# The first stage of a fused attention and feed-forward kernel, in 256-token chunks

## What is computed

```python
xn = layernorm(x)
q_c  = rms_norm(xn @ wq_down.T, q_norm_w)       # 1536 wide
kv_c = rms_norm(xn @ wkv_down.T, kv_norm_w)     # 512 wide
k_rope = rope(xn @ wk_rope.T)                   # 64 wide
q, k, v = up-projections of q_c and kv_c, 16 heads
s = softmax(causal(q k^T * scale)) v @ wo.T
g = silu(down(silu(gate(xn) * gate_s) * (up(xn) * up_s)) * down_s)
out = x + s * g
```

## Time and profile before

| | us |
|---|---|
| runs shown (3) | 4663.2, 4666.9, 4667.2; median 4666.9 |
| the profiled execution | 4694.8 |
| its span, slowest core (7) | 4693.3 |
| first stage on that core | 0 to 573.4 |
| its first matmul | 94.8 |

### The profile page before, as it was taken

One profiled execution on the slowest core, in us unless ns is written; L12 is line 12 of the kernel. 1 busy time (PEld: TensorE's weight loads), 2 busy tenths in 40 slices (PEclk: granted clock), 3 DMA queues, 4 the chain that ended last, 5 costly groups with the idle time before them and its releaser, 6 DMA issues.

```text
span 4693.3 us, 57615 instructions; the slowest of 8 cores (4635.0 to 4693.3 us)
## 1 busy us (share of the span) xinstructions
PE 3775.5 (80%) x22128; PEld 1896.8 (40%) x22128; DVE 1598.3 (34%) x3298; ACT 1205.3 (26%) x1751; POOL 365.6 (8%) x455
## 2 busy tenths in 40 slices
PE   1777796766676667756775999999799999999998
PEld 0333343444344444434442444444344444444443
DVE  2444335665565556655673111110000111110100
ACT  1222104544454445545552000000000111000000
POOL 0111230000000000000000000000000100000101
PEclk9887798998898888988998999999899999999999
DMA  8555246787878787788777344445655443434564
GB/s 180 137 139 139 61 110 104 116 116 115 101 121 116 116 109 119 111 106 113 121 118 180 72 78 75 78 74 176 190 189 194 84 81 72 81 72 135 175 197 157
DMA packets 778331, 566.60 MB, mean 121 GB/s; under 512 B 689232, under 2 KB 697680, under 8 KB 766928
## 3 DMA queue, kind: packets, MB, share of 16 engines
q1 hardware_dynamic: 711840, 318.04, 35.3%
q0 software_dynamic: 37424, 171.46, 20.2%
q10 hardware_dynamic: 28800, 73.41, 5.1%
HBM read 499.34 MB, written 73.40 MB: 122 GB/s over the span
## 4 chain that ended last, share of the span: by engine, by line
PE 65%; DMA 16%; DVE 12%; issue 3%; ACT 2%; another core or an unknown queue 1%; SPq 0%; POOL 0%; ACTq 0%; DVEq 0%; POOLq 0%
PE bk L1065 25%; PE bk L1085 11%; DMA pt<-pp 8%; DVE nmx L895 6%; PE bk L1104 5%; PE ps_mm L427 4%; PE ps_u L829 4%; PE ps_o L883 3%; PE ps_s L862 3%; DMA dw<-d 3%; PE ps_s L865 3%; PE ps_kv L427 2%; PE ps_u L834 2%; PE ps_r L665 2%; DMA xt<-xn 2%
## 5 line engine op out<-in xcount | busy, mean ns | idle before, releaser
L939 ACT ACTIVATE pp<-ps_s,bia,scq 128x1024 bf16<-128x1024 f32 (+3 forms) x640 | 690.1, 1078 | 861.0 <-DMA pt<-pp 345.6
L895 DVE TENSOR_REDUCE nmx<-ps_s 128x1 f32<-128x1024 f32 (+3 forms) x640 | 680.3, 1063 | 665.8 <-PE ps_s L869 436.5
L883 PE MATMUL ps_o<-vv,pt 128*128 128x129 bf16 x4352 | 370.1, 226 | 471.8 <-DMA pt<-pp 327.6
L1065 PE MATMUL bk<-xc,gw 128*128 128x512 bf16 x2816 | 643.0, 382 | 48.5 <-DMA uw<-upP 48.5
L1085 PE MATMUL bk<-dw,hdn 128*128 128x512 bf16 x2816 | 616.7, 381 | 56.1 <-DMA dw<-d 53.9
L1065 PE MATMUL bk<-xc,uw 128*128 128x512 bf16 x2816 | 636.5, 379 | 0.0
L883 PEld LDWEIGHTS ps_o<-vv,pt 128*128 128x128 bf16 x4352 | 287.0, 100 | 631.9 <-issue 607.4
L1121 DVE SCALAR_TENSOR_TENSOR hdn<-bk,us_s,sg 128x512 bf16<-128x512 f32 x176 | 132.1, 751 | 1137.7 <-PE bk L1065 1061.5
L1085 PEld LDWEIGHTS bk<-dw,hdn 128*128 128x128 bf16 x2816 | 275.8, 98 | 395.1 <-issue 69.2
L1065 PEld LDWEIGHTS bk<-xc,gw 128*128 128x128 bf16 x2816 | 276.9, 98 | 386.1 <-issue 58.2
L862 PE MATMUL ps_s<-kk,qn 128*128 128x512 bf16 (+3 forms) x1280 | 349.2, 355 | 97.0 <-ACT fac L944 86.8
(11 more groups left out here) (101 smaller groups left out, 2696.2 us busy)
## 6 DMA issues: line engine op xcount, KB each, us to landing
dw<-d SPq DMA_DIRECT2D x176, 512.0 KB, 4.6
gw<-gateP POOLq DMA_DIRECT2D x88, 512.0 KB, 5.1
uw<-upP POOLq DMA_DIRECT2D x88, 512.0 KB, 7.1
xb<-xk ACTq DMA_DIRECT2D x32, 1024.0 KB, 6.4
wo_s<-wo SPq DMA_DIRECT2D x16, 2048.0 KB, 9.6
d<-downP POOLq DMA_DIRECT2D x16, 1408.0 KB, 22.1
xo<-xk ACTq DMA_DIRECT2D x64, 256.0 KB, 4.9
out<-xo ACTq DMA_DIRECT2D x64, 256.0 KB, 6.1
```

Of the source, the lines that this page charges most:

```text
L883: mm_ = e.matmul(ps_o[n % 2][:, 0:129], pt[n % NPT][:, j * 128:(j + 1) * 128], V[:, kt, 0:129], start=(j == 0), stop=(j == 2 * nt - 1))
L895: kb.go(e, lambda: e.tensor_reduce(nmx[n % 8][:], r3(ps_s[n % 2][:], 2)[:, :, 0:w], AX.XY, ALU.max, negate=True), [("p", f"b_s_{n}")], "v")
L939: kb.go(e, lambda: e.activation(r3(pp[n % NP][:, 0:2 * w], 2), r3(ps_s[n % 2][:], 2)[:, :, 0:w], AF.Exp, bias=bia[n % 8][:], scale=scq[:, ...
L1065: mm_ = e.matmul(bk[pr * 2 + z][:], W[u_i % 2][:, dc * 128:(dc + 1) * 128], xc[hf][:, dc * 512:(dc + 1) * 512], start=(dc == 0), stop=(dc ...
```

## The change

The chunks of the first stage become 256 tokens wide, 16 in number, two tiles each. `CSEQ` starts with two kv-only chunks and then alternates, with two own chunks at the end. There are four `xt`, three `xb`. Layer norm runs three chunks ahead: six tiles stand before the first job, and chunk n carries the tiles of chunk n + 3. A query or kv job makes two groups of 128 outputs side by side in one bank, 16 matmuls of 256 columns each, so a job still has 512 columns of result; own chunks have 6 query jobs, all have 2 kv jobs and a rope job of 256 columns. The kv squares are summed by TensorE over two accumulators rather than added by POOL. The statistics are handed on from chunk to chunk, one event behind each job: a kv-only chunk carries qc and qd of the own chunk before and its own kc; its kd and ka follow the first and second job of the next chunk; an own chunk has kc after its rope job, kd after the fourth query job, ka after the fifth. `rb` is the same buffer as `dg`. SP loads x, the constants and the rotary factors, x first; a later x load stands on SP behind the transpose of the tile three before. The query weights come in six pieces, each with a semaphore of its own. Stores to DRAM are in pieces of 256 tokens, 512 bytes each. VectorE waits for the constants only where it needs them.

```diff
-    w["wqd"] = _tiles(a(inputs["L0_attn_wq_down"]).T, 128, QR)
+    w["wqd"] = _tiles(a(inputs["L0_attn_wq_down"]).T, 128, 256)
...
-            xb = [sb(f"xb{i}", [128, D], F32) for i in range(2)]
+            xb = [sb(f"xb{i}", [128, D], F32) for i in range(NX)]
             xn = [sb(f"xn{i}", [128, D], BF16) for i in range(2)]
-            xt = [sb(f"xt{i}", [128, NDC * 512], BF16) for i in range(2)]
...
-            acck = sb("acck", [128, 512], F32)
+            acck = [sb(f"acck{i}", [128, 512], F32) for i in range(2)]
             accq = sb("accq", [128, 512], F32)
-            cs = [sb(f"cs{i}", [128, 512], F32) for i in range(2)]
-            dg = sb("dg", [128, 512], F32)
-            rb = sb("rb", [128, 512], F32)
...
-            CSEQ = [0, 4, 1, 5, 2, 6, 3, 7]
+
+            CSEQ = [8, 9, 0, 10, 1, 11, 2, 12, 3, 13, 4, 14, 5, 15, 6, 7]
+            NC = len(CSEQ)
+            LNS = 2 * NC
 
             def sched():
                 ev = []
-                for t in range(4):
-                    ev += [("L1", 0, t), ("L2", 0, t)]
+                for n in range(3):
+                    for t in range(2):
+                        ev += [("L1", n, t), ("L2", n, t)]
+                late = []
                 for n, c in enumerate(CSEQ):
...
+                    jobs = ([("q", 0), ("q", 1), ("q", 2), ("kv", 0), ("kv", 1), ("kr", 0),
+                             ("q", 3), ("q", 4), ("q", 5)] if c < 8 else [("kv", 0), ("kv", 1), ("kr", 0)])
+                    todo = []
+                    if n + 3 < NC:
+                        for t in range(2):
+                            todo += [[("L1", n + 3, t)], [("L2", n + 3, t)]]
+                    stats, late = late, []
                     for j, job in enumerate(jobs):
                         ev.append(("job", n, job))
...
+                        if job == ("kr", 0):
+                            stats += [("kc", n), ("kd", n), ("ka", n)]
+                        for _ in range(2 if c >= 8 else 1):
+                            if todo:
+                                ev += todo.pop(0)
+                        if stats:
+                            ev.append(stats.pop(0))
+                    for left in todo:
+                        ev += left
+                    late = stats + ([("qc", n), ("qd", n)] if c < 8 else [])
+                return ev + late
...
                 if job[0] == "kv":
-                    return ps_kv[job[1]]
+                    return ps_kv[(n % 2) * 2 + job[1]]
...
             def a_sync(e):
+                def load(tt):
+                    row = CSEQ[tt // 2] * 256 + (tt % 2) * 128
+                    kb.inc(e.dma_start(out=xb[tt % NX][:], in_=xk_d[row:row + 128, :]), f"xb{tt % NX}", 16)
+                    kb.mark(f"a_x_{tt}", f"xb{tt % NX}")
...
+                for tt in range(NX):
+                    load(tt)
...
+                load_cs(0)
+                load_cs(1)
                 for ev_ in EV:
+                    if ev_[0] == "job" and ev_[2][0] == "kr" and 0 < ev_[1] < NC - 1:
+                        kb.wait(e, "v", f"a_kro_{ev_[1] - 1}")
+                        load_cs(ev_[1] + 1)
                     if ev_[0] != "L2":
                         continue
                     _, n, t = ev_
-                    sl = (n * 4 + t) % 2
+                    tt = n * 2 + t
                     kb.wait(e, "a", f"a_xn_{n}_{t}")
-                    kb.wait(e, "p", f"a_jobs_{n - 2}")
-                    kb.wait(e, f"xst{((n - 2) // 2) % 2}", f"a_xst_{n - 2}")
-                    xt_ = f"xt{n % 2}{t}"
+                    kb.wait(e, "p", f"a_jobs_{n - 4}")
+                    kb.wait(e, f"xst{(n // 2) % 2}", f"a_xst_{n - 4}")
+                    xt_ = f"xt{n % 4}{t}"
                     kb.inc(e.dma_start_transpose(
-                        out=r3(xt[n % 2][:], NDC)[:, :, t * 128:(t + 1) * 128],
-                        in_=xn[sl][:]), xt_, 16)
+                        out=r3(xt[n % 4][:], NDC)[:, :, t * 128:(t + 1) * 128],
+                        in_=xn[tt % 2][:]), xt_, 16)
                     kb.mark(f"a_xt_{n}_{t}", xt_)
+                    if tt + NX < LNS:
+                        load(tt + NX)
...
-                H = NDC * QR // 4
-                for z in range(4):
-                    kb.inc(e.dma_start(out=wqd[:, z * H:(z + 1) * H], in_=wqd_d[:, z * H:(z + 1) * H]),
-                           "wa1", 16)
-                kb.mark("a_wq", "wa1")
+                H = NDC * 256
+                for z in range(6):
+                    kb.inc(e.dma_start(out=wqd[:, z * H:(z + 1) * H], in_=wqd_d[z * 128:(z + 1) * 128, :]),
+                           f"wq{z}", 16)
+                    kb.mark(f"a_wq_{z}", f"wq{z}")
                 for ev_ in EV:
                     if ev_[0] == "job":
                         _, n, job = ev_
...
+                        if r == 2:
+                            for t in range(2):
+                                kb.wait(e, f"xt{n % 4}{t}", f"a_xt_{n}_{t}")
+                            c = CSEQ[n]
+                            dst = r3(xnscr[(c // 2) * 128:(c // 2 + 1) * 128, :], NDC)
+                            s_ = f"xst{(n // 2) % 2}"
+                            kb.wait(e, s_, f"a_xst_{n - 4}")
+                            kb.inc(e.dma_start(out=dst[:, :, (c % 2) * 256:(c % 2 + 1) * 256],
+                                               in_=r3(xt[n % 4][:], NDC)), s_, 16)
+                            kb.mark(f"a_xst_{n}", s_)
...
                         if job[0] == "q":
-                            kb.wait(e, "wa1", "a_wq")
+                            kb.wait(e, f"wq{job[1]}", f"a_wq_{job[1]}")
                         if job[0] == "kv":
-                            kb.wait(e, "v", f"a_ka_{n - 1}")
+                            kb.wait(e, "v", f"a_ka_{n - 2}")
...
+                        X = xt[n % 4]
+                        for z in range(1 if job[0] == "kr" else 2):
+                            for dc in range(NDC):
+                                if job[0] == "kv":
+                                    k0 = dc * KVR + (job[1] * 2 + z) * 128
+                                    wt = wkvd[:, k0:k0 + 128]
+                                elif job[0] == "kr":
+                                    wt = wkr[:, dc * 128:(dc + 1) * 128]
+                                else:
+                                    k0 = job[1] * NDC * 256 + dc * 256 + z * 128
+                                    wt = wqd[:, k0:k0 + 128]
+                                mm_ = e.matmul(bk[:, z * 256:(z + 1) * 256], wt, X[:, dc * 256:(dc + 1) * 256],
+                                               start=(dc == 0), stop=(dc == NDC - 1))
...
+                        if ev_[0] == "kc":
+                            kb.wait(e, "a", f"a_sq_{n}_kv_1")
+                            parts = [(acck[0], 0), (acck[0], 1), (acck[1], 0), (acck[1], 1)]
                         else:
-                            kb.wait(e, "a", f"a_rb_{n - 1}")
-                            kb.wait(e, "v", f"a_qu_{n - 1}")
-                        for tt in range(4):
-                            mm_ = e.matmul(ps_st[:, tt:tt + 1], acc[:, tt * 128:(tt + 1) * 128], ones[:, 0:1],
-                                           start=True, stop=True)
+                            kb.wait(e, "g", f"a_add_{n}_5")
+                            parts = [(accq, 0), (accq, 1)]
+                        for tt in range(2):
+                            for k, (acc, z) in enumerate(parts):
+                                k0 = z * 256 + tt * 128
+                                mm_ = e.matmul(ps_st[:, tt:tt + 1], acc[:, k0:k0 + 128], ones[:, 0:1],
+                                               start=(k == 0), stop=(k == len(parts) - 1))
...
                     elif ev_[0] == "kd":
                         n = ev_[1]
+                        kb.wait(e, *stat_done[ev_])
                         kb.wait(e, "v", f"a_dg_{n}")
-                        kb.inc(e.matmul(ps_st[:], ones[:], dg[:], start=True, stop=True), "p")
+                        kb.inc(e.matmul(ps_st[:, 0:256], ones[:], dg[:], start=True, stop=True), "p")
...
-                kb.wait(e, "qc", "a_consts")
...
-                            kb.go(e, lambda: e.tensor_scalar(
-                                qraw[:, r * OWN + c * 512:r * OWN + (c + 1) * 512], bk[:], qnw[:, r:r + 1],
-                                None, ALU.mult, ALU.bypass),
-                                [("a", f"a_sq_{n}_q_{r}")], "v", f"a_ev_{(n,) + job}")
+                            dst = r3(qraw[:], NRQ)[:, 2 * r:2 * r + 2, c * 256:(c + 1) * 256]
+                            wt = qnw[:, 2 * r:2 * r + 2].unsqueeze(2).broadcast_to([128, 2, 256])
+                            kb.go(e, lambda: e.tensor_tensor(dst, r3(bk[:], 2), wt, ALU.mult),
+                                  [("a", f"a_sq_{n}_q_{r}")], "v", f"a_ev_{(n,) + job}")
...
+                        kb.wait(e, "qc", "a_consts")
```

(30 more changed lines are left out.)

164 lines of the change are left out of this document (59 added, 105 removed).

## The result

The changed kernel takes 4709.3 us (median of four runs, 4703.1 to 4715.6) where the kernel before, timed beside it, takes 4667.0 (4663.2 to 4672.0): ratio of the two 1.009, interval 1.0072 to 1.0109. It is slower, by 42 us where 22 were forecast, and just above the range's end of 4706. A second timing gave 1.012 (1.0101 to 1.0139). Some executions of these kernels are slow, with the cores of one die or both at a lower granted clock and the time some per cent longer; ratios and times compare the others.

What follows compares the result with a forecast made beforehand. It took the first stage to be held by TensorE's waits for transposed rows (155.1 us) and the scale (34.9). Its terms summed to +21.9 us, giving 4688.8 on the median of 4666.9; range 4658 to 4706.

Steps and rivals of the forecast that it cites:

- waits for rows: TensorE's three later first-stage waits for transposed rows, before query chunks, would go: -60.3 us.
- 256-column matmuls: First-stage matmuls, 1408 of 512 columns becoming 2816 of 256, would cost nearly the same in all: +1.5 us.
- float32 sums: TensorE's sums of squares in the first stage would grow from 96 to 320 float32 rows: +22.7 us.
- waits for the scale, and the end: Sixteen kv scale chains would leave TensorE waiting, +38.6 us; a shorter tail behind the last kv sums, -7.8 us.
- clock: TensorE's clock would fall to 1.2 GHz behind 15 scale waits, where 10 waits did so before: +14.6 us.
- start: Tiles made ahead and x loads behind transposes would delay the first query chunk to 129 us: +12.6 us.
- rival C: Weight loads show behind the 256-column matmuls: +87 us, 4776 with the rest; chance 0.03.
- Rival B: x loads queue behind transposes on SP, 11 us per tile, first query chunk 20 us later: 4709; chance 0.10, shared.
- Rival D: At the start transposes get through beside the weights, first query chunk near 113: -16 us, 4673; chance 0.10.
- The change touches only the first stage: Only the first stage, up to 573.4 us, was read; everything behind it was taken as unchanged.
- near 595: Sign that the forecast is right: the next stage starts near 595 us, where it started at 573.4 before.
- Rival A: The clock holds in the nine scale waits of 3.5 us: -21.6 us, leaving +0.3, 4667; chance 0.20.

Runs made afterwards that it cites:

- the version with the later sums: Changed kernel with statistics events ahead of layer norm events, and the scale's broadcast and the square sums each one job later: 4583.4 to 4595.0 us, ratio 0.9767.
- statistics first: Changed kernel with the statistics event before the layer norm events behind each job, not after: ratio 1.0011.
- GpSimd's add: Changed kernel with POOL adding the second kv accumulator to the first, so TensorE sums 8 float32 rows a chunk, not 16: ratio 1.0027.
- both remedies: The version with the later sums, plus GpSimd's add of the second key accumulator to the first: ratio 0.978.

## Why the prediction was right and wrong

The sign and the mechanism held: rows stop being waited for, and scale chains, float32 sums and a clock that falls behind each short wait cost more. By the sum's own terms, forecast and measured from core 0 before to core 1 after:

| term | forecast | measured |
|---|---|---|
| waits for rows | -60.3 | -59.9 (153.2 - 93.3, to none) |
| 256-column matmuls | +1.5 | +3.4 (2816 x 0.1092 - 1408 x 0.216) |
| float32 sums | +22.7 | +24.5 (320 x 0.107 - 96 x 0.101) |
| waits for the scale, and the end | +30.8 | +22.8 |
| clock | +14.6 | +27.3 (55.2 busy, less the two rows on matmuls and sums) |
| start | +12.6 | +3.9 (first matmul -13.1, waits 13.9 and 3.1) |
| sum | +21.9 | +22.0 |

- *Rows.* Right, and why, too: the pair of chunks leaves them time enough, with room to spare (44.7 us in the version with the later sums).
- *Matmuls.* Right; rival C is out. The Trainium skill has a second figure in the same section (TensorE: Matmul & The Clock Gate, Back-to-back issue gap), N / 2.4 + 2.5 ns for a single matmul; worked out for 256 columns, an estimate, that is 109.2 ns. The trace agrees with that one (0.109 us), in a sustained stream of loads and matmuls, and not with the 131 ns for 512 columns (216 here). No stream here has 128 columns, so the 81 ns stand untested.
- *Scale.* The waits came out as worked out: 6 of 6.00 (6.2 forecast), 8 of 3.44 (3.5), 2.94, the start's 3.14, and six of 0.6: 73.4 in all against 73.5, and 70.3 without the start's, which I had not counted here. What the row is off by lies in the base: core 0 before had 43.6 of them, not the 34.9 that I read on core 7 up to 560, without the last chain.
- *Clock.* The step that failed inside the stage. I counted 15 falls by waits of 3.5 us and more; on core 1 the trace has 20 stretches at 1.2 GHz between 130 and 565 (core 0 before: 10 up to 540, as counted). Fourteen are those I counted; behind the wait of 2.94 the clock held. Six stand behind the sums that follow a wait of 0.6 us, which I had priced as a wait alone; each makes the 32 matmuls behind it take 5.32 in place of 3.65, 10 us together. With the float32 broadcast in it, a fall behind 3.44 cost 2.9, not 2.4. Some 4 us more of the measured row lie in the start: from 80.2 to 124.2 TensorE is busy for 27.0 us, where the same work at full clock is some 21.4 (160 matmuls, 32 rows of float32, one broadcast), and before the change the slow clock behind the first matmul cost only some 1.4. I had put 2 us for this into the start.
- *Start.* Too dear by 9 us. First matmul 80.2 (near 80 forecast), first query product 124.2 (129), so 5 of the 9 us are real and the others stand in the clock's row. Tiles came 6.5 us apart, not 7.0. Rival B is out, and it is the other way round: SP's queue is the better one. Rival D, 113, did not come.
- *What was not in the sum.* "The change touches only the first stage" failed, and this step took the time out of the range: I had put everything behind the stage at nothing, and it is 12 us longer (4109 against 4097), nearly all in the attention stage, whose instructions are the same. Inside the stage the sum was met by luck: the clock is 12.7 too low, start and scale 8.7 and 8.0 too high, and these cancel. The stage's own loss is +17 in the mean of undisturbed cores and +22 between these two. That leaves some 13 of the 42 us, and they are open. They are not the step from the mean of the cores to the slowest: that is 21.7 us in the four runs of the changed kernel and 20.7 in the thirteen runs of the kernel before that were timed with the last experiments and count. I had put one profile's difference onto the median as if nothing behind the stage could move.
- *What was to be seen.* The next stage did not start near 595 but at 576.4: I added +22 to a core 7 that its stretch at 0.81 had made 14 us late against the mean of the undisturbed cores. As a base for that time it was wrong.
- *Rival A* had 0.20. It came true in part, on three cores of one profile and behind some waits of 3.44 with GpSimd's add. I had tied it to waits under 3 us, and no row bears that out: the clock held and fell behind 3.44, held behind 2.94 and fell behind 0.64. It is not a question of the length of the wait alone.

The change was not a bad one. With its buffers and chunks the first stage is 108 us shorter (558.9 to 451.3) once sums and broadcast each stand one job behind what feeds them and layer norm runs two chunks ahead; as ordered, it hands all of that back. Not all 108 are the chunks' own: the later broadcast alone gave the kernel before 16.5.

## What to carry to other kernels

When a stage is cut finer, every chain from TensorE over two other engines and back is run more often: put each of its steps at least one job behind the one that feeds it, and look in the order of all engines for what stands ahead of it, a normalisation of 2.1 us as well as a tile's statistics. Price a short wait of TensorE by the matmuls behind it as well: here 10.1 us of waits a pair came to 17.5 with the clock behind them. Take the base of a sum from several cores, and look at the clock of each first.

## What was not expected of the hardware

- The clock fell behind a wait of 0.64 us followed by 16 float32 sums (0.67 in the 5.2 us behind them), but not in the pairs of the version with the later sums, with a wait of 0.75 us and the same sums elsewhere (1.00). The same wait of 3.44 us was followed by a fall on one core and not on another, in one execution. With statistics first, core 1 ran at 1.00 from 279.7 to 330.7 through waits of 3.44, 2.01 and 2.94, and in the next pair the clock fell behind waits of the same three lengths.
- Some cores have stretches in the first stage, 117 to 161 us in all, at a granted clock between the two levels (0.81), always pairs of neighbouring cores, from one pair to three in a profile. In the profile with both remedies it cost a core some 19 us (stage ends of 475.9 to 481.5 against 457.5 to 460.5), in the first profile of the kernel before 13.
- Loads of x on a second queue beside the transposes go with 14.5 us to landing for these in place of 8.4.
